# Last half of a fused attention and feed-forward kernel: the product with proj and the attention of the first half one slot sooner, each transpose directly behind its addition

## The chip, the core and the metric

The kernel runs on one core of a Trainium2 chip. The core has five engines with instruction streams of their own, which meet only through semaphores: PE (TensorE, matrix products into PSUM), DVE (VectorE), ACT (ScalarE), POOL (GpSimd) and SP (SyncE), which issues most of the DMAs. ACT issues four DMAs as well, at the very end. The metric is the device time of one execution in microseconds (us). Lower is better.

## The reference

```python
x = L0_attn_x                                   # (8, 1024, 256) float32
xn = _layernorm(x)                              # over the last axis, no weights
# attention, 16 heads of 16 channels, no softmax
qkv = xn @ qkv_w + qkv_b
q, k = l2norm(q), l2norm(k)                     # over the 16 channels of a head
kv  = einsum('bhnd,bhne->bhde', k, v)           # 16x16 for each head and batch
out = einsum('bhnd,bhde->bhne', q, kv)          # heads joined again: (8, 1024, 256)
attn = out @ proj_w + proj_b
# feed-forward, 256 -> 1024 -> 256
ffn = relu(xn @ W1 + b1) @ W2 + b2
return x + attn + ffn
```

## The kernel before

The 8 batches of 1024 tokens are worked through in 16 halves of 512 tokens; half `s` is the half `u = s % 2` of batch `b`. Every float32 factor is split into a high and a low part of type fp32r, and a product is three matmuls (`product`, L1006 to L1008): high by high, low by high, high by low. So most tiles come as a pair `_hi`, `_lo`: ACT makes the high part (L460, L523) and DVE subtracts it to get the low one (L677, L818).

The feed-forward part of a half runs over 8 chunks `j` of the 1024 inner channels. `ffn_up(j)` multiplies into `w_bank[j % 2]`; ACT takes the relu as `h_hi` (`h_high`), DVE the rest as `h_lo` (`h_low`); `ffn_down(j)` multiplies these by W2 into the output banks. PE's order is one list of slots written by hand: slot `j` holds `ffn_up(j + 2)`, then `ffn_down(j)`, then what else stands at that `j`. In the last half (`ahead` is false) `ffn_down` is `ffn_down_last`, 12 matmuls with 256 columns into `o_bank[0]`, `o_bank[1]` and `v_bank[0]`.

The attention has no softmax, so the tokens are summed first. `gather` (slot 2) accumulates xn^T k in `g_bank`, `key_value` multiplies it by the v weights into `kv_bank`, and DVE masks it to the blocks of the heads (`mask_kv`, L827 to L833 and L677). `project` multiplies that by proj into `g_bank`; `m_high` on ACT and `m_low` on DVE split the result into `m_hi` and `m_lo`. `attend(b, u, banks)` multiplies m by the transposed q of a half; one signal (`o_ready`) follows each of its two channel chunks.

In the last half `attend(b, 0, w_bank)` puts the attention of the batch's first half into the two `w_bank`s, which `ffn_up` no longer needs by then. It waits for `h_lo_done` of all 8 chunks, since `h_low` reads these banks, for `m_lo_done` and for `qT_lo_done`. After slot 7, `attend_last` adds the attention of the second half to the feed-forward sums in the output banks.

At the end DVE finishes both halves. For the first: `add_attention` (L845) adds the two `w_bank`s to what ACT had laid down of the feed-forward part, `spread_y` (L857) transposes 32x32 blocks into `y_rows`, `add_rows` (L863) adds them to x in `y_sb`. ACT then issues four stores (L668) of 128 KB each, one after the other; each covers 32 partitions in short pieces. For the second half: `add_last` (L871) adds the three output banks to `y_sb` as they come ready, and SP issues a store of 256 KB (L350) and two of 128 KB (L353). SP waits for all the stores before the kernel ends.

All five programs follow the same walk over the halves (`all_batches`). Six batches run in a loop on each engine; the first and the last are written out, so what is conditional on `ahead` or `last` touches only the last half.

Of the kernel before, what the change touches and what calls it, by code (L numbers as in the profile page):

```python
# [50 lines left out]
KC = C // P  # L51
# [11 lines left out]
def build(nc, x, qkv_w, qkv_b, proj_w, proj_b, w1, b1, w2, b2, out):  # L63
# [6 lines left out]
    with ctx:  # L70
# [140 lines left out]
        def is_first(s):  # L211
            return isinstance(s, int) and s == 0
# [245 lines left out]
        def _(act):  # L458
# [38 lines left out]
            def qk_out(s, u, t):  # L497

                wait(act, qk_ready, TILES * s + t + 1)
                wait(act, qk_ss_done, TILES * s + t - 1)  # L500
                nc.scalar.activation(qk_sq[:, t % 2, :], v_bank[t % 2][:], ACT.Square).then_inc(qk_sq_done, 1)  # L501
                if t == 0:
                    wait(act, q_transposed, s - 1)
                    wait(act, k_lo_done, s - 1)
                    if is_first(s):
                        act.wait_ge(wqk_ready, 1)
                    elif is_second(s):
                        act.wait_ge(w2_ready, PARTS)
                copy(qk[u][:, t, :], v_bank[t % 2][:]).then_inc(qk_copied, 1)
# [10 lines left out]
            def h_high(s, j):  # L520

                wait(act, h_ready, JC * s + j + 1)
                nc.scalar.activation(h_hi[:, j % RING, :], w_bank[j % 2][:], ACT.Relu).then_inc(h_done, 1)  # L523
# [92 lines left out]
            def half(b, s, u, last):  # L616
                ahead = not (last and u == 1)
                if not is_second(s):
                    h_high(s, 2)
                k_high(s, u)  # L620
                h_high(s, 3)
                if ahead:
                    qk_out(s + 1, 1 - u, 0)
                h_high(s, 4)
                if not last:
                    ln_sqrt(s + 2)
                    normalise(s + 2, u)
                if u == 1:
                    g_high(b)
                if not last:  # L630
                    xn_high(s + 2, u)
                h_high(s, 5)
                if ahead:
                    qk_out(s + 1, 1 - u, 1)
                h_high(s, 6)
                if is_second(s):
                    qT_high(0, 0)
                if ahead:
                    qT_high(s, u)
                    qk_out(s + 1, 1 - u, 2)  # L640
                h_high(s, 7)
                if ahead:
                    qk_out(s + 1, 1 - u, 3)
                    h_high(s + 1, 0)
                    qk_sqrt(s + 1)
                if u == 1:
                    m_high(b)
                if ahead:
                    h_high(s + 1, 1)
                    if u == 0:  # L650
                        yT_out(b, 0, 0)
                        yT_out(b, 0, 1)
                else:
                    qT_high(s, u)
                if not last:
                    xT_high(s + 2, u)
# [17 lines left out]
        def _(dve):  # L674
# [140 lines left out]
            def h_low(s, j):  # L815
                r = j % RING
                wait(dve, h_done, JC * s + j + 1)
                nc.vector.scalar_tensor_tensor(h_lo[:, r, :], w_bank[j % 2][:], 0.0, h_hi[:, r, :].bitcast(F32),  # L818
                                               ALU.max, ALU.subtract).then_inc(h_lo_done, 1)
# [5 lines left out]
            def mask_kv(b):  # L825
                wait(dve, kv_ready, b + 1)
                nc.vector.tensor_copy(kv[:], kv_raw[:, :, 0, :]).then_inc(kv_half_done, 1)  # L827
                wait(dve, kv_half_done, b + 1)
                nc.vector.tensor_tensor(kv[:], kv_raw[:, :, 1, :], kv[:], ALU.add).then_inc(kv_sum_done, 1)
                wait(dve, kv_sum_done, b + 1)  # L830
                nc.vector.tensor_tensor(kv[:], kv[:], head_mask[:], ALU.mult).then_inc(kv_masked, 1)
                wait(dve, kv_masked, b + 1)
                nc.vector.tensor_copy(kv_hi[:], kv[:]).then_inc(kv_hi_done, 1)  # L833
                wait(dve, kv_hi_done, b + 1)
                less(kv_lo[:], kv[:], kv_hi[:]).then_inc(kv_done, 1)
# [5 lines left out]
            def add_attention(b, k, last):  # L841

                wait(dve, o_ready, (2 * b * KC) + k + 1)
                wait(dve, yT_copied, KC * 2 * b + k + 1)
                nc.vector.tensor_tensor(yT[0][:, k, :], (w_bank if last else v_bank)[k][:], yT[0][:, k, :],  # L845
                                        ALU.add).then_inc(yT_added, 1)
# [87 lines left out]
            def half(b, s, u, last):  # L934
                ahead = not (last and u == 1)
                if not is_second(s):
                    if ahead:
                        xT_low(s + 1, 1 - u)
                    h_low(s, 2)
                divide(0, u, q_done)  # L940
                if is_second(s):
                    k_low(s, u)
                    h_low(s, 3)
                    transpose_q(s, u)
                else:
                    transpose_q(s, u)
                    h_low(s, 3)
                    k_low(s, u)
                if not last:
                    variance(s + 2, b + 1, u)  # L950
                h_low(s, 4)
                if ahead:
                    sum_squares(s + 1, 0)
                if not last:
                    spread(s + 2)
                if u == 1:
                    g_low(b)
                if not last:
                    transpose_x(s + 2)
                h_low(s, 5)  # L960
                if ahead:
                    sum_squares(s + 1, 1)
                else:
                    mask_kv(b)
                h_low(s, 6)
                if is_second(s):
                    qT_low(0, 0)
                if ahead:
                    qT_low(s, u)
                    sum_squares(s + 1, 2)  # L970
                    if u == 1:
                        mask_kv(b)
                h_low(s, 7)
                if ahead:
                    sum_squares(s + 1, 3)
                    bound(s + 1)
                    h_low(s + 1, 0)
                    norms(s + 1)
                if u == 1:
                    m_low(b)  # L980
                if ahead:
                    h_low(s + 1, 1)
                    divide(1, 1 - u, k_done)
                else:
                    qT_low(s, u)

            def end(b, last):
                for k in range(KC):
                    add_attention(b, k, last)
                for k in range(KC):  # L990
                    spread_y(b, 0, k)
                if last:
                    add_rows(b)
                    add_last(b)
                    return
                for k in range(KC):
                    spread_y(b, 1, k)
# [5 lines left out]
        def _(pe):  # L1003
# [199 lines left out]
            def half(b, s, u, last):  # L1203
                ahead = not (last and u == 1)
                for j in range(JC):
                    if j + AHEAD < JC:
                        ffn_up(s, u, j + AHEAD)
                    elif ahead:
                        ffn_up(s + 1, 1 - u, j + AHEAD - JC)
                    ffn_down(s, b, u, j, last)  # L1210
                    if j == 6 and not ahead:
                        pe.wait_ge(h_lo_done, JC * (s + 1))
                        attend(b, 0, w_bank)
                    if j == 1 and ahead:
                        query_key(s + 1, 1 - u, 0, b)
                    if j == 2:
                        gather(s, b, u)
                    if j == 3 and ahead:
                        query_key(s + 1, 1 - u, 1, b)
                    if j == 4 and ahead:  # L1220
                        query_key(s + 1, 1 - u, 2, b)
                    if j == 5 and ahead:
                        query_key(s + 1, 1 - u, 3, b)
                    if j == (4 if ahead else 3) and u == 1:
                        if isinstance(b, int) and b == 0:
                            pe.wait_ge(wvp_ready, 2)
                        key_value(b)
                    if j == (6 if ahead else 5) and u == 1:
                        project(b)

            def end(b, last):
# [27 lines left out]
```

## Time and profile before

| | us |
|---|---|
| median of 3 runs | 575.96 (575.56 to 576.06) |
| the profiled execution | 576.76 |
| its span, first to last instruction | 575.0 |
| PE busy | 560.1 (97%) |
| DVE busy | 416.6 (72%) |
| ACT busy | 282.6 (49%) |
| mean granted clock of PE | 0.997 of full speed |

A span is one execution as the hardware profiler saw it. A row of the timeline gives a start, a duration, the engine, the line and the operation. Matmuls are pipelined, so the start of one lies before the end of the one ahead of it: 0.39 us is the duration of a matmul of 512 columns, and one starts every 0.23 us. ACTq and SPq are the queues in which these engines issue DMAs; the duration of such a row is the issue and not the transfer. "To landing" counts from the start of the issue to the completion signal. Queue q10 is ACT's, q1 is SP's.

### The profile page before, as it was taken

To read this page: it belongs to the slowest core of one execution; us is meant where nothing else is said; L and a number is where in the kernel's file an instruction comes from. 1 tells how busy PE (TensorE), PEld (TensorE's weight loads), DVE (VectorE), ACT (ScalarE), POOL (GpSimd) and SP (SyncE) were. 2 spreads that over 40 slices of the span, in tenths; PEclk is the share of its full clock that TensorE was granted. 3 is DMA by queue.
4 is the path that set the end of the run, shared out by engine and by line. 5 is a ranking of instruction groups with operands and counts; after the bars stand their busy time and mean duration, and the time that the engine had idled before them with its cause. 6 is when DMAs were issued, how large, how long until landed. Compare 5 with 4: busy or idle time off the path is not lost.

```text
span 575.0 us, 8950 instructions
## 1 busy us (share of the span) xinstructions
PE 560.1 (97%) x2722; PEld 474.6 (83%) x2722; DVE 416.6 (72%) x807; ACT 282.6 (49%) x516; POOL 119.8 (21%) x147
## 2 busy tenths in 40 slices
PE   7999988999999999999999999999999999999995
PEld 6788767888888888888888888888888888888895
DVE  6888668767787677868678596776778767783744
ACT  3487273455535554355633645445554555533420
POOL 2338022310242010520205202132024301050100
PEclk9999999999999999999999999999999999999998
DMA  8303235144333536135451453514434252515323
GB/s 284 120 36 73 42 82 99 34 101 81 85 70 80 103 60 113 17 85 94 85 94 20 85 94 84 82 32 98 80 90 65 43 103 37 92 22 90 89 38 74
DMA packets 141398, 45.36 MB, mean 79 GB/s; under 512 B 133314, under 2 KB 136386, under 8 KB 141380
## 3 DMA queue, kind: packets, MB, share of 16 engines
q1 hardware_dynamic: 139264, 44.61, 38.4%
q10 hardware_dynamic: 2116, 0.53, 0.5%
q8 instruction: 9, 0.15, 0.1%
q14 instruction: 9, 0.07, 0.1%
HBM read 20.98 MB, written 8.39 MB: 51 GB/s over the span
## 4 chain that ended last, share of the span: by engine, by line
PE 84%; DVE 6%; SPq 5%; ACT 1%; DMA 1%; issue 1%; DVEq 0%; ACTq 0%
PE o_bank L1006 10%; PE o_bank L1007 10%; PE o_bank L1008 10%; PE w_bank L1008 9%; PE w_bank L1006 9%; PE w_bank L1007 9%; PE v_bank L1006 6%; PE v_bank L1007 6%; PE v_bank L1008 5%; SPq L305 5%; PE g_bank L1006 3%; PE g_bank L1008 3%; PE g_bank L1007 3%; DMA qT_lo<-blocks 1%; PE kv_bank L1127 1%
## 5 line engine op out<-in xcount | busy, mean ns | idle before, releaser
L818 DVE SCALAR_TENSOR_TENSOR h_lo<-w_bank,h_hi 128x512 fp32r<-128x512 f32 x128 | 87.4, 683 | 37.6 <-ACT h_hi L523 36.1
L523 ACT ACTIVATE h_hi<-w_bank 128x512 fp32r<-128x512 f32 x128 | 76.5, 597 | 72.4 <-PE w_bank L1008 70.4
L1006 PE MATMUL w_bank<-xT_hi,w_hi 128*128 128x512 f32 x254 | 99.9, 393 | 1.5 <-DVE h_lo L818 1.5
L1008 PE MATMUL w_bank<-xT_hi,w_lo 128*128 128x512 f32 x254 | 100.0, 394 | 0.0
L1007 PE MATMUL w_bank<-xT_lo,w_hi 128*128 128x512 f32 x254 | 99.7, 393 | 0.0
L368 POOL TENSOR_TENSOR xn_lo<-xn,xn_hi 128x256 fp32r<-128x256 f32 x60 | 44.6, 743 | 242.8 <-ACT xn_hi L460 239.3
L1006 PE MATMUL o_bank<-h_hi,w_hi 128*128 128x512 f32 x240 | 94.9, 395 | 0.0
L1007 PE MATMUL o_bank<-h_lo,w_hi 128*128 128x512 f32 x240 | 94.7, 395 | 0.0
L1008 PE MATMUL o_bank<-h_hi,w_lo 128*128 128x512 f32 x240 | 94.6, 394 | 0.0
L383 POOL TENSOR_TENSOR y_sb<-y_sb,y_rows 128x256 f32<-128x256 f32 x56 | 53.0, 951 | 127.6 <-DVE y_rows L857 108.1
L501 ACT ACTIVATE qk_sq<-v_bank 128x512 f32<-128x512 f32 x64 | 38.4, 599 | 77.9 <-PE v_bank L1008 76.8
L785 DVE TENSOR_REDUCE qk_v<-qk_sq 128x32 f32<-128x512 f32 x64 | 43.4, 681 | 33.5 <-ACT qk_sq L501 33.3
L1006 PEld LDWEIGHTS w_bank<-xT_hi,w_hi 128*128 128x128 f32 x254 | 47.7, 188 | 11.7 <-DVE h_lo L818 2.1
L1008 PEld LDWEIGHTS w_bank<-xT_hi,w_lo 128*128 128x128 f32 x254 | 47.7, 188 | 10.2
L1007 PEld LDWEIGHTS w_bank<-xT_lo,w_hi 128*128 128x128 f32 x254 | 47.7, 188 | 9.3
L1007 PEld LDWEIGHTS o_bank<-h_lo,w_hi 128*128 128x128 f32 x240 | 46.9, 195 | 9.4
L1006 PEld LDWEIGHTS o_bank<-h_hi,w_hi 128*128 128x128 f32 x240 | 46.5, 194 | 9.5
L1008 PEld LDWEIGHTS o_bank<-h_hi,w_lo 128*128 128x128 f32 x240 | 46.7, 195 | 9.2
L1006 PE MATMUL v_bank<-wqk_hi,xT_hi 128*128 128x512 f32 x128 | 50.6, 396 | 1.7 <-issue 1.5
L1007 PE MATMUL v_bank<-wqk_lo,xT_hi 128*128 128x512 f32 x128 | 50.3, 393 | 0.0
L1008 PE MATMUL v_bank<-wqk_hi,xT_lo 128*128 128x512 f32 x128 | 50.0, 391 | 0.0
L476 ACT ACTIVATE xn<-x_sb,ln_offset,ln_rstd 128x256 f32<-128x256 f32 x56 | 29.1, 590 | 27.9 <-DVE ln_offset L729 27.9
(183 smaller groups left out, 983.0 us busy)
## 6 DMA issues: line engine op xcount, KB each, us to landing
qT_lo<-blocks SPq DMA_DIRECT2D x256, 32.0 KB, 1.9
x_sb<-x SPq DMA_DIRECT2D x15, 512.0 KB, 3.8
y_sb<-x SPq DMA_DIRECT2D x60, 128.0 KB, 3.4
out<-y_sb SPq DMA_DIRECT2D x58, 128.0 KB, 2.7
xT_raw<-blocks SPq DMA_DIRECT2D x224, 32.0 KB, 1.9
y_sb<-w SPq DMA_DIRECT2D x4, 256.0 KB, 5.3
w_raw<-w SPq DMA_DIRECT2D x1, 768.0 KB, 9.5
x_sb<-x SPq DMA_DIRECT2D x2, 256.0 KB, 2.8
```

Source lines behind the costliest of these rows:

```text
L305: sp.dma_start(to_pairs[j * BLOCK:(j + 1) * BLOCK, :, g * run:(g + 1) * run], by_row[g * BLOCK:(g + 1) * BLOCK, j]).then_inc(moved, 16)
L368: nc.gpsimd.tensor_tensor(xn_lo[:, u, t, :], xn_of(s)[:, t, :], xn_hi[:, u, t, :].bitcast(F32), ALU.subtract).then_inc(xn_split_done, 1)
L383: nc.gpsimd.tensor_tensor(y_sb[:, u, t, :], y_sb[:, u, t, :], y_rows[:, u, t, :], ALU.add).then_inc(y_done, 1)
L476: done = nc.scalar.activation(to[:, t, :], x_sb[:, u, t, :], ACT.Identity, bias=ln_offset[:, t:t + 1], scale=ln_rstd[:, t:t + 1])
L501: nc.scalar.activation(qk_sq[:, t % 2, :], v_bank[t % 2][:], ACT.Square).then_inc(qk_sq_done, 1)
L523: nc.scalar.activation(h_hi[:, j % RING, :], w_bank[j % 2][:], ACT.Relu).then_inc(h_done, 1)
L785: nc.vector.tensor_reduce(qk_v[:, t, :], qk_sq[:, t % 2, :].rearrange("p (h d) -> p h d", d=D), AXIS.X, ALU.add).then_inc(qk_ss_done, 1)
L818: nc.vector.scalar_tensor_tensor(h_lo[:, r, :], w_bank[j % 2][:], 0.0, h_hi[:, r, :].bitcast(F32), ALU.max, ALU.subtract).then_inc(h_lo_do ...
L1006: nc.tensor.matmul(to, left[0], right[0], start=first, stop=False, skip_group_check=shared)
L1007: nc.tensor.matmul(to, left[0], right[1], start=False, stop=False, skip_group_check=shared)
L1008: return nc.tensor.matmul(to, left[1], right[0], start=False, stop=last, skip_group_check=shared)
L1127: nc.tensor.matmul(kv_raw[:, g, :, :], wv_hi[:, k, heads], g_parts[:, k, :, heads], start=g == 0 and k == 0, stop=False, skip_group_check= ...
```

## The change

In the last half alone, three programs are reordered.

```diff
@@ scalar: half
+                if not ahead:
+                    m_high(b)
                 h_high(s, 7)
...
-                if u == 1:
+                if u == 1 and ahead:
                     m_high(b)
@@ vector: half
+                if not ahead:
+                    m_low(b)
                 h_low(s, 7)
...
-                if u == 1:
+                if u == 1 and ahead:
                     m_low(b)
@@ vector: end
-                for k in range(KC):
-                    add_attention(b, k, last)
-                for k in range(KC):
-                    spread_y(b, 0, k)
+                if last:
+                    for k in range(KC):
+                        add_attention(b, k, last)
+                        spread_y(b, 0, k)
+                else:
+                    for k in range(KC):
+                        add_attention(b, k, last)
+                    for k in range(KC):
+                        spread_y(b, 0, k)
@@ tensor: half
-                    if j == 6 and not ahead:
+                    if j == 5 and not ahead:
                         pe.wait_ge(h_lo_done, JC * (s + 1))
                         attend(b, 0, w_bank)
...
-                    if j == (6 if ahead else 5) and u == 1:
+                    if j == (6 if ahead else 4) and u == 1:
                         project(b)
```

No instruction is added or taken away. On PE, this is the end of slot 4 of the last half and what follows it, before. The first row is the last matmul of `ffn_down(4)`, the next six are `ffn_up(7)`, and the last row begins `ffn_down(5)`.

```order
L1008 MATMUL v_bank0<-w2_hi,h_lo 128x256
L1006 MATMUL w_bank1<-xT_hi,w1_hi 128x512 [waits h_lo_done]
L1007 MATMUL w_bank1<-xT_lo,w1_hi 128x512
L1008 MATMUL w_bank1<-xT_hi,w1_lo 128x512
L1006 MATMUL w_bank1<-xT_hi,w1_hi 128x512
L1007 MATMUL w_bank1<-xT_lo,w1_hi 128x512
L1008 MATMUL w_bank1<-xT_hi,w1_lo 128x512
L1006 MATMUL o_bank0<-w2_hi,h_hi 128x256 [waits h_lo_done]
```

The same place on PE in the changed kernel:

```order
L1017 MATMUL v_bank0<-w2_hi,h_lo 128x256
L1015 MATMUL g_bank<-proj_hi,kv_hi 128x256 [waits kv_done]
L1016 MATMUL g_bank<-proj_lo,kv_hi 128x256
L1017 MATMUL g_bank<-proj_hi,kv_lo 128x256
L1015 MATMUL g_bank<-proj_hi,kv_hi 128x256
L1016 MATMUL g_bank<-proj_lo,kv_hi 128x256
L1017 MATMUL g_bank<-proj_hi,kv_lo 128x256
L1015 MATMUL w_bank1<-xT_hi,w1_hi 128x512 [waits h_lo_done]
```

The six matmuls of `project` now stand ahead of `ffn_up(7)` and `ffn_down(5)`. In the same way the 12 matmuls of `attend` have moved from behind `ffn_down(6)` to directly behind `ffn_down(5)`.

On ACT, the end of the program as a difference (`h_hi` rows are `h_high`, the row with `m_hi` is `m_high`):

```order
-L523 ACTIVATE h_hi<-w_bank 128x512 [waits h_ready] x3
+L523 ACTIVATE h_hi<-w_bank 128x512 [waits h_ready] x2
 L460 ACTIVATE m_hi<-g_bank 128x512 [waits m_ready]
-L460 ACTIVATE qT_hi<-qT_lo 128x512 [waits q_moved]
-L460 ACTIVATE qT_hi<-qT_lo 128x512
-L668 DMA out<-y_sb 32x16x64 [waits y_done]
-L668 DMA out<-y_sb 32x16x64 x3
+L523 ACTIVATE h_hi<-w_bank 128x512 [waits h_ready]
+L460 ACTIVATE qT_hi<-qT_lo 128x512 [waits q_moved]
```

One `h_high`, that of chunk 7, has gone behind `m_high`. The other rows only moved with it.

On DVE, the end of the program before, from `kv_lo` on; `h_lo` x2 are chunks 6 and 7:

```order
L677 TENSOR_TENSOR kv_lo<-kv,kv_hi 128x256 [waits kv_hi_done]
L818 SCALAR_TENSOR_TENSOR h_lo<-w_bank,h_hi 128x512 [waits h_done] x2
L677 TENSOR_TENSOR m_lo<-g_bank,m_hi 128x512 [waits m_hi_done]
L677 TENSOR_TENSOR qT_lo<-qT_lo,qT_hi 128x1024 [waits qT_hi_done]
L845 TENSOR_TENSOR xn_first<-w_bank,xn_first 128x512 [waits yT_copied,o_ready] x2
L857 STREAM_TRANSPOSE y_rows<-xn_first 128x512 [waits y_done,yT_added]
L857 STREAM_TRANSPOSE y_rows<-xn_first 128x512 [waits yT_added]
L863 TENSOR_TENSOR y_sb<-y_sb,y_rows 128x1024 [waits yT_spread,y_loaded0]
```

And in the changed kernel:

```order
L679 TENSOR_TENSOR kv_lo<-kv,kv_hi 128x256 [waits kv_hi_done]
L820 SCALAR_TENSOR_TENSOR h_lo<-w_bank,h_hi 128x512 [waits h_done]
L679 TENSOR_TENSOR m_lo<-g_bank,m_hi 128x512 [waits m_hi_done]
L820 SCALAR_TENSOR_TENSOR h_lo<-w_bank,h_hi 128x512 [waits h_done]
L679 TENSOR_TENSOR qT_lo<-qT_lo,qT_hi 128x1024 [waits qT_hi_done]
L847 TENSOR_TENSOR xn_first<-w_bank,xn_first 128x512 [waits yT_copied,o_ready]
L859 STREAM_TRANSPOSE y_rows<-xn_first 128x512 [waits y_done,yT_added]
L847 TENSOR_TENSOR xn_first<-w_bank,xn_first 128x512 [waits yT_copied,o_ready]
L859 STREAM_TRANSPOSE y_rows<-xn_first 128x512 [waits yT_added]
L865 TENSOR_TENSOR y_sb<-y_sb,y_rows 128x1024 [waits yT_spread,y_loaded0]
```

`m_low` now stands between the two `h_low`, and the first transpose between the two additions.

## Rows read from the trace of the kernel before

**Rows 1.** The page's chain of work that ended last, by engine.

```profile
PE 84%; DVE 6%; SPq 5%; ACT 1%; DMA 1%; issue 1%; DVEq 0%; ACTq 0%
```

**Rows 2.** Timeline of the queues: start, duration of the issue, queue, line.

```profile
545.31 10.87 SPq L305 DMA_DIRECT2D qT_lo<-blocks  x16
...
568.15 0.38 ACTq L668 DMA_DIRECT2D out<-y_sb  x1
...
568.75 0.38 SPq L350 DMA_DIRECT2D out<-y_sb  x1
...
569.65 1.36 ACTq L668 DMA_DIRECT2D out<-y_sb  x1
...
569.70 1.34 SPq L353 DMA_DIRECT2D out<-y_sb  x1
```

**Rows 3.** Stores: queue, count, KB each, median us to landing; last row: those of 569.65 and 569.70.

```profile
out<-y_sb SPq DMA_DIRECT2D x58, 128.0 KB, 2.7
...
out<-y_sb ACTq DMA_DIRECT2D x1, 128.0 KB, 2.2
...
out<-y_sb SPq DMA_DIRECT2D x1, 256.0 KB, 3.3
...
DMA to landing us min/median/max: 4.7/4.9/5.0
```

**Rows 4.** DMA queues, 569 to 575: packets, MB, share of 16 engines' time.

```profile
q10 hardware_dynamic: 2112, 0.52, 50.4%
q1 hardware_dynamic: 432, 0.52, 25.4%
```

**Rows 5.** Busy time of each engine by stretch, granted clock, DMA share, GB/s.

```profile
569.00:569.50 0.50, 0.16 (x2) 0.00 (x0) 0.35 (x2) 0.00 (x0) 0.00 (x0) 1.00 0.78 130
...
569.50:573.50 4.00, 0.00 (x0) 0.00 (x0) 0.12 (x1) 0.00 (x0) 0.00 (x0) 0.69 0.99 234
```

**Rows 6.** Timeline of PE: start, duration, line, operation.

```profile
556.68 0.39 PE L1006 MATMUL w_bank<-xT_hi,w_hi 128*128 128x512 f32 x1
...
559.50 0.28 PE L1006 MATMUL g_bank<-proj_hi,kv_hi 128*128 128x256 f32 x1
...
561.51 0.28 PE L1008 MATMUL v_bank<-w_hi,h_lo 128*128 128x256 f32 x1
561.81 0.47 PE L1006 MATMUL w_bank<-qT_hi,m_hi 128*128 128x512 f32 x1
...
568.88 0.28 PE L1008 MATMUL v_bank<-m_hi,qT_lo 128*128 128x256 f32 x1
```

**Rows 7.** Timeline of DVE; in brackets idle time before and its releaser.

```profile
555.71 0.42 DVE L677 TENSOR_TENSOR kv_lo<-kv,kv_hi 128x256 fp32r<-128x256 f32 x1
...
558.89 0.69 DVE L818 SCALAR_TENSOR_TENSOR h_lo<-w_bank,h_hi 128x512 fp32r<-128x512 f32 x1 [2.12 <-ACT h_hi L523]
561.02 0.69 DVE L677 TENSOR_TENSOR m_lo<-g_bank,m_hi 128x512 fp32r<-128x512 f32 x1 [1.44 <-ACT m_hi L460]
...
563.48 0.69 DVE L845 TENSOR_TENSOR xn_first<-w_bank,xn_first 128x512 f32<-128x512 f32 x1 [0.20 <-PE w_bank L1008]
564.88 0.69 DVE L845 TENSOR_TENSOR xn_first<-w_bank,xn_first 128x512 f32<-128x512 f32 x1 [0.71 <-PE w_bank L1008]
565.49 1.30 DVE L857 STREAM_TRANSPOSE y_rows<-xn_first 128x512 f32<-128x512 f32 x2
566.89 1.23 DVE L863 TENSOR_TENSOR y_sb<-y_sb,y_rows 128x1024 f32<-128x1024 f32 x1
...
569.20 0.42 DVE L871 TENSOR_TENSOR y_sb<-v_bank,y_sb 128x256 f32<-128x256 f32 x1
```

**Rows 8.** Timeline of ACT, its last rows that are no DMA.

```profile
558.25 0.60 ACT L523 ACTIVATE h_hi<-w_bank 128x512 fp32r<-128x512 f32 x1 [2.21 <-PE w_bank L1008]
560.39 0.60 ACT L460 ACTIVATE m_hi<-g_bank 128x512 fp32r<-128x512 f32 x1 [1.53 <-PE g_bank L1008]
560.88 1.14 ACT L460 ACTIVATE qT_hi<-qT_lo 128x512 fp32r<-128x512 f32 x2
```

## The prediction

> **What bounds the kernel now.** I read the chain of waits first. It is 84% PE [rows 1], and PE is busy 97% of the span (the table above), so as long as matmuls are left, every other engine is cover. The change adds and removes no matmul. So the question is whether it shortens a wait of PE, or the stretch behind the last matmul, in which PE is no longer the bound.
>
> Then the timeline of PE at the end. Between the last matmul of `ffn_down(6)` at 561.51 and the first of `attend` at 561.81 lie 0.30 us, where such matmuls otherwise start 0.12 apart: (561.51 - 559.50) / 17 = 0.118 for the 18 from `project` on. PE waits 0.18 us there. DVE shows for what: `m_lo` runs from 561.02 to 561.71, and `attend` starts 0.10 later [rows 6, 7]. PE's last matmul starts at 568.88 and DVE's last addition at 569.20; it ends at 569.62 [rows 6, 7].
>
> Behind that there is only DMA. SP issues its last store at 569.70, ACT its last one at 569.65 [rows 2]; they take 4.7 and 5.0 us to landing [rows 3], so they land at 574.40 and 574.65. The span ends at 575.0, 0.4 behind the later one. 5.4 of the 575 us are thus a tail without a matmul. Is that the price of one store? No: a store of SP takes 2.7 us as the median of 58, and ACT's first one, with nothing before it, took 2.2 [rows 3]. From 569.5 to 573.5 the 16 DMA engines are 0.99 busy [rows 5]. All the seven last stores stand in line there: the four of ACT, issued from 568.15 on [rows 2], with 2112 small packets and 50.4% of six us, and the three of SP with 432 packets and 25.4% [rows 4]. That is 3.02 + 1.52 = 4.55 us of work for all the engines together. It starts at about 569.1 (0.78 of 569.0 to 569.5 is busy [rows 5]), 0.95 us after ACT's first issue, and so is worked off at 573.65 at the earliest. The tail is bound by the amount that is left to store when PE ends, and two thirds of it belong to the first half, whose result is complete long before.
>
> **The change, part by part.**
>
> 1. `project` goes from behind `ffn_down(5)` to before `ffn_up(7)`. It takes the place at 556.68 instead of 559.50 [rows 6], 2.82 sooner. It needs `kv_lo`, which ends at 555.71 + 0.42 = 556.13 [rows 7]; 0.55 us are to spare. Cost 0, and a stall of PE for whatever `kv_lo` is later than that.
>
> 2. `ffn_up(7)` and `ffn_down(5)` slide back by the six matmuls of `project`, 6 x 0.118 = 0.7 us. `m_hi` on ACT moves with `project`: 560.39 - 2.82 = 557.57, and ends at 558.17. `h_hi` of chunk 7 moves from 558.25 to 558.95 [rows 8], so it doesn't wait for `m_hi` though it now stands behind it. On DVE `m_lo` runs from 558.20 to 558.89, `h_lo` of chunk 7 from 558.89 + 0.7 = 559.59 to 560.28 [rows 7]. No wait here either.
>
> 3. `attend` goes from behind `ffn_down(6)` to behind `ffn_down(5)`. Before, `ffn_down(5)` ended where `project` began, at 559.50; now it ends at 560.20. `attend` waits for three things. `m_lo` is there at 558.89, 1.3 us early: the old wait is gone. What is late next is `h_lo` of chunk 7, at 560.28. With the 0.10 us that the signal took before, `attend` starts at 560.38, and PE waits 0.18 us again, as much as before. The price of this wait lies between 0 (the signal is as fast as PE's own queue) and 0.5 (if ACT and DVE take 0.3 longer for that chunk, which is about half an operation of 0.60). I take 0.18, so the balance of PE is 0 and its last matmul still starts at 568.88. Behind `attend` stand the 24 matmuls of slots 6 and 7 and `attend_last`. The latter needs `qT_lo` of the second half: `qT_hi` follows `h_hi` at 559.55 (its moves were issued by 545.31 + 10.87 = 556.18 [rows 2]) and ends at 560.69, `qT_lo` takes 1.23 and is done at about 561.96, 4 us before it is needed.
>
> 4. `attend` is 561.81 - 560.38 = 1.43 us sooner, and so are both `o_ready`. The first addition moves from 563.48 to 562.05, just behind `qT_lo`. The second would start at 564.88 - 1.43 = 563.45 [rows 7].
>
> 5. The first transpose goes between them. Two transposes take 1.30 together [rows 7], so one 0.65 to 0.69. The first addition ends at 562.74, the transpose runs until 563.45 at the latest: it fits into the 0.71 us in which DVE waited for PE before the second addition [rows 7]. The second addition ends at 564.14, its transpose at about 564.85. `add_rows` started 0.10 behind the transposes (566.79 and 566.89 [rows 7]), so now at 564.95, and ends at 566.18 instead of 568.12: 1.94 us sooner, 1.43 from `attend` and 0.5 from the hidden transpose. The page "VectorE: DVE Perf Modes" of the Trainium skill, section "The DRAIN you can't avoid", speaks against this order: a DVE instruction doesn't start until the pipeline behind the one before is empty. Here the second addition and the transposes that didn't depend on it stand 565.49 - 564.88 = 0.61 apart with 0.69 of busy time each, so the trace shows some overlap where nothing is waited for. By the rule nothing is lost in the new order; by the rows up to 0.1 for each dependent pair, and that is in the times above.
>
> 6. ACT's four stores are issued from 566.2 on instead of 568.15. No other edit touches the tail. SP's first store comes 0.3 us sooner too, since `add_last` no longer stands behind `add_rows` when its first bank is ready; its last one stays at 569.70, bound by PE.
>
> **What the tail becomes.** The packets start 0.95 behind the first issue, now at 567.1. The 4.55 us of work would be done at 571.7 if nothing ran dry. SP's last store can't begin to move before about 569.70 + 0.95 = 570.65; by then ACT's 3.0 us of work, begun at 567.1, is nearly all out. So the end is that of a nearly undisturbed store of 128 KB: 2.2 us to landing at the least, 2.7 at the median, 3.3 as SP's 256 KB store took in the middle of the jam [rows 3]. That gives a landing at 571.9, 572.4 or 573.0, and with the 0.4 behind it a span of 572.3, 572.8 or 573.4. The gains are 2.7, 2.2 and 1.6 us. I take the median store's, 2.2: it is the row for the same queue and size, and it agrees with the work's end at 571.7 plus the 0.6 to 1.0 that landing took behind 573.65 before.
>
> The page "DMA: Bandwidth & Descriptors", section "Issuing engines are not separate DMA queues", says that DMAs from any engine run on the same 16 engines and interleave. The trace agrees: both queues' packets share the stretch in which the DMA share is 0.99 [rows 5]. Were the rings separate, ACT's load would not have slowed SP's last store, and the gain would be that of the second rival. The same page, section "Latency and other measured facts", adds that the completion of a write is shorter when HBM is lightly loaded; no row here separates that part.
>
> Sum: 576.76 of the profiled execution - 2.2 = 574.5. It lay 0.8 above the median of the runs, 575.96. From the median I get 573.7.
>
> **Rivals.**
>
> *The jam dissolves only in part.* ACT's last issue took 1.36 us against 0.38 for the first [rows 2]; if the four issues are slow by themselves, the last packets of the first half meet SP's last store. Then that one lands after the mean of 3.3 and 4.7, 4.0 us: 573.7, span 574.1, gain 0.9, time 575.0. Against it: SP's issues were as slow at the same moment (1.34), so the delay is shared and comes from the jam.
>
> *The last store's 4.7 us are its own.* Then only ACT's later landing falls away: the end goes from 574.65 to 574.40, gain 0.25, time 575.7. For it speaks that the clock of the tail is set by a row that does not move (569.70). Against it are 2.2 and 2.7 for stores of the same size.
>
> *PE stalls more: slower.* `attend` now comes one slot behind `ffn_up(7)` where it came two behind, and the way over ACT and DVE has no slack left. The place is the `h_lo` wait; every us there moves PE's last matmul and SP's last store with it. With the gain of the tail at 2.2, it decides from 2.2 us on; to be 1.2 slower in the end it would need 3.4. The nearest rows make 0.5 of it at most. Only if the tail gave nothing, and `kv_lo` and `h_lo` both came an operation late (0.42 + 0.69 us over their slack), would the time be 576.8.
>
> *It doesn't do what it says.* If `y_done` came less than 1 us sooner (an addition that waits for `qT_lo`, with 0.09 us to spare in step 4), the tail would still shrink by nearly as much. This is within the first rival.
>
> **Chances.** The measurement of this kernel can tell about 0.2%, 1.15 us, from no change. The forecast, a gain of 1.6 to 2.7, has 0.74. The first rival, 0.6 to 1.6, has 0.15, of which I count 0.1 as faster. The second has 0.08. The slower case has 0.03. That makes 0.85 faster (with what lies above 2.7), 0.12 within 0.2% and 0.03 slower. The range goes from 2.7, the bound, with 0.35 us for the scatter of the runs (half of what lies between 575.56 and 576.06, and a little more), 572.9, to the first rival's 575.0.
>
> **What would show it.** PE: `project` starting near 556.7 without a gap, `attend` near 560.4 behind a gap of about 0.2, `attend_last` ending where it did, at 569.2. DVE: the first transpose between the additions, `add_rows` ending near 566.2. ACTq: the first store near 566.2 and the last by 568.5. DMA: the engines busy from 567.1 on, well below 0.9 after 571, and SP's last store 2.2 to 3.3 us to landing. The forecast is wrong if that one still takes over 4 us, if the last landing is not SP's, or if PE's end has moved by more than 0.3.

## The result and the profile after

| | before | after |
|---|---|---|
| median of 11 runs, us | 576.38 (575.56 to 577.11) | 574.49 (573.93 to 575.21) |
| the profiled execution | 576.76 | 573.93 |
| its span | 575.0 | 572.2 |

The ratio is 0.9968, with an interval from 0.9960 to 0.9976. The changed kernel is faster by 1.84 us, with 1.4 to 2.3 in the interval; the forecast was 2.2. The time of 574.49 lies 0.8 above the forecast 573.7: half of that is the smaller gain, and the other half is that the kernel before itself came out at 576.38 here and not at the 575.96 that the forecast started from. The two spans are 2.8 us apart, which is more than the change made. About 1.05 of that was there long before the last half: the first sums of squares of q and k on DVE start at 34.12 in one trace and at 32.98 in the other, the first matmul of the third half's `gather` at 107.34 and 106.30, and at the end of slot 4 of the last half the two traces are still 1.05 apart. So times of the two traces are compared from a common place: the end of `ffn_down(4)`, 556.68 before [rows 6] and 555.63 after.

The timeline of PE after: start, duration, line, operation.

```profile
555.63 0.28 PE L1015 MATMUL g_bank<-proj_hi,kv_hi 128*128 128x256 f32 x1
...
556.32 0.39 PE L1015 MATMUL w_bank<-xT_hi,w_hi 128*128 128x512 f32 x1
...
559.02 0.28 PE L1017 MATMUL v_bank<-w_hi,h_lo 128*128 128x256 f32 x1
559.27 0.51 PE L1015 MATMUL w_bank<-qT_hi,m_hi 128*128 128x512 f32 x1
559.62 0.39 PE L1016 MATMUL w_bank<-qT_lo,m_hi 128*128 128x512 f32 x1
...
567.81 0.28 PE L1017 MATMUL v_bank<-m_hi,qT_lo 128*128 128x256 f32 x1
```

`project` starts without a gap. `attend` starts 3.64 us behind the common place; before it was 561.81 - 556.68 = 5.13 [rows 6], so it is 1.49 sooner. In front of it there is again a gap, 0.25 from start to start where 0.12 is usual, and its first matmul holds the next back by 0.35 instead of 0.23. The last matmul lies 12.18 us behind the common place, and 12.20 before: PE has gained nothing.

The same stretch on DVE:

```profile
557.15 0.69 DVE L679 TENSOR_TENSOR m_lo<-g_bank,m_hi 128x512 fp32r<-128x512 f32 x1 [1.42 <-ACT m_hi L460]
558.52 0.69 DVE L820 SCALAR_TENSOR_TENSOR h_lo<-w_bank,h_hi 128x512 fp32r<-128x512 f32 x1 [0.68 <-ACT h_hi L523]
559.56 1.23 DVE L679 TENSOR_TENSOR qT_lo<-qT_lo,qT_hi 128x1024 fp32r<-128x1024 f32 x1 [0.35 <-ACT qT_hi L460]
560.98 0.69 DVE L847 TENSOR_TENSOR xn_first<-w_bank,xn_first 128x512 f32<-128x512 f32 x1 [0.19 <-PE w_bank L1017]
561.70 0.71 DVE L859 STREAM_TRANSPOSE y_rows<-xn_first 128x512 f32<-128x512 f32 x1
562.38 0.69 DVE L847 TENSOR_TENSOR xn_first<-w_bank,xn_first 128x512 f32<-128x512 f32 x1
563.11 0.72 DVE L859 STREAM_TRANSPOSE y_rows<-xn_first 128x512 f32<-128x512 f32 x1
563.93 1.23 DVE L865 TENSOR_TENSOR y_sb<-y_sb,y_rows 128x1024 f32<-128x1024 f32 x1
...
568.13 0.42 DVE L873 TENSOR_TENSOR y_sb<-v_bank,y_sb 128x256 f32<-128x256 f32 x1 [0.29 <-PE v_bank L1017]
```

The first addition and the first transpose fill the 1.40 us between the starts of the two additions; before, 0.71 of them were idle [rows 7]. `add_rows` ends at 565.16, 9.53 behind the common place instead of 11.44: 1.91 sooner.

The issues of the stores, ACT's four together and the last of SP:

```profile
565.18 2.24 ACTq L670 DMA_DIRECT2D out<-y_sb  x4
...
567.48 0.38 SPq L350 DMA_DIRECT2D out<-y_sb  x1
567.91 1.48 SPq L353 DMA_DIRECT2D out<-y_sb  x2
```

And how SP's two stores of 128 KB (line 353) fared, from the view of that line:

```profile
DMA to landing us min/median/max: 3.0/3.1/3.2
```

The last of the two, issued at 568.69, is the one with 3.0 us to landing, against 4.7 [rows 3]. I call the time from the end of DVE's last addition to the end of the span the **tail**, and the time from the end of `add_rows` to the end of DVE's last addition the **lead** that the first half's stores have. Before, the lead was 1.50 us and the tail 5.41 (with the span of 575.03, which is 575.0 when rounded); now they are 3.39 and 3.65. The tail is 1.76 us shorter, and that is the whole gain. The other tails below are taken from spans rounded to 0.1 us, so each is good to 0.05.

### The profile page after: what moved, and what is told of

It is laid out like the page before. It is cut to its first block, busy times and chain, and to the rows that moved or that the text cites. A ratio compares the mean times of both kernels' runs of the same rounds, so it can differ in the third digit from the quotient of the medians.

```text
span 572.2 us, 8950 instructions
## 1 busy us (share of the span) xinstructions
PE 560.6 (98%) x2722; PEld 475.7 (83%) x2722; DVE 415.2 (73%) x807; ACT 282.7 (49%) x516; POOL 119.4 (21%) x147
## 4 chain that ended last, share of the span: by engine, by line
PE 84%; DVE 6%; SPq 5%; ACT 2%; issue 1%; DMA 1%; DVEq 0%; ACTq 0%
PE o_bank L1015 10%; PE o_bank L1016 10%; PE o_bank L1017 10%; PE w_bank L1017 9%; PE w_bank L1015 9%; PE w_bank L1016 9%; PE v_bank L1015 6%; PE v_bank L1016 6%; PE v_bank L1017 6%; SPq L305 5%; PE g_bank L1015 3%; PE g_bank L1017 3%; PE g_bank L1016 3%; PE kv_bank L1136 1%; DVE ln_parts L707 1%
```

## The experiments

All ratios are to the kernel before, run beside it on the same chip. The diffs are against the changed kernel, and the minus lines are its lines, if nothing else is said.

**e1: the slots alone.**

```diff
-                if last:
-                    for k in range(KC):
-                        add_attention(b, k, last)
-                        spread_y(b, 0, k)
-                else:
-                    for k in range(KC):
-                        add_attention(b, k, last)
-                    for k in range(KC):
-                        spread_y(b, 0, k)
+                for k in range(KC):
+                    add_attention(b, k, last)
+                for k in range(KC):
+                    spread_y(b, 0, k)
```

> The changed kernel with the two additions and then the two transposes on DVE, as before; project and attend stay one slot sooner. Jam theory (the tail is as long as the stores of both halves take to drain, so it shrinks by 0.9 us for each us that the first half's result comes sooner, 1.76 / 1.94 in the profiles of the two kernels): the addition of x and y_rows ends 1.4 us sooner instead of 1.94, the gain over the kernel before is 1.3 us, ratio 0.9977. Floor theory (with the first half out of the way SP's last store is the end by itself, and 1.4 us are already enough): the gain is the whole 1.8 us of the changed kernel, ratio 0.9968, and SP's last store lands 3.2 us after its issue.

Ratio 0.9971 (0.9961 to 0.9982). The interval holds the values of both theories, but the profile tells them apart. These rows are `add_rows` and DVE's last addition; the span is 573.8:

```profile
565.72 1.23 DVE L865 TENSOR_TENSOR y_sb<-y_sb,y_rows 128x1024 f32<-128x1024 f32 x1
...
569.46 0.42 DVE L873 TENSOR_TENSOR y_sb<-v_bank,y_sb 128x256 f32<-128x256 f32 x1 [0.29 <-PE v_bank L1012]
```

The lead is 2.93, the tail 3.92. It has not reached the 3.65 of the changed kernel, and SP's two stores of 128 KB took 3.4 and 3.6 us to landing instead of 3.2 at most, so there was no floor yet. For 1.43 us more lead than before the tail gave 1.49.

**e2: the transposes alone** (the kernel before with the `if last` branch that e1 takes out).

> The kernel before with the first transpose between the two additions; project and attend stay where they were. Jam theory: the first transpose fits into the 0.71 us in which DVE waited for PE, the addition of x and y_rows ends 0.5 us sooner, the gain is 0.45 us, ratio 0.9992, and e1 and e2 add up to the changed kernel. Floor theory: 0.5 us here as well, but e1 and e2 together give more than the changed kernel. If the transposes cost more behind their additions than they hide: no gain.

Ratio 0.9998 (0.9990 to 1.0007): the expected 0.9992 is inside, no change as well; the runs can't tell. In the profile DVE places the transpose between the additions as in the changed kernel (additions at 562.70 and 564.10, transpose at 563.43), the lead grows to 1.96, and the tail is 4.96: 0.45 less, the expected amount. That is a single profile, and the runs neither confirm nor refute it.

**e3: `m_high` and `m_low` behind chunk 7 again**, with PE's order as changed.

```diff
-                if not ahead:
-                    m_high(b)
                 h_high(s, 7)
...
-                if u == 1 and ahead:
+                if u == 1:
                     m_high(b)
```

and the same for `m_low`.

> The changed kernel with m_high and m_low behind h_high and h_low of chunk 7 again on ACT and DVE; PE's order stays changed. If this order matters as the row arithmetic has it: m_lo ends 0.65 us later than attend now starts, PE waits 0.8 us instead of 0.13, its last matmul and SP's last store are 0.65 later and so is the first half's result; the gain over the kernel before falls from 1.8 to 1.1 us, ratio 0.998. If ACT and DVE have cover there: no difference from the changed kernel, ratio 0.9968.

Ratio 0.9986 (0.9977 to 0.9994). PE's last matmul of `ffn_down(5)` and the first of `attend`:

```profile
559.28 0.28 PE L1013 MATMUL v_bank<-w_hi,h_lo 128*128 128x256 f32 x1
560.18 0.48 PE L1011 MATMUL w_bank<-qT_hi,m_hi 128*128 128x512 f32 x1 [0.62 <-issue]
```

The gap is 0.90 instead of 0.25. From `h_lo` of chunk 6 to the last matmul it takes 13.40 us, against 12.78 in the changed kernel (555.03 to 567.81). So PE lost 0.62. The gain fell from 1.8 to 0.8 us, with 0.3 to 1.3 in its interval; the expected 1.1 is inside, and so is what the profile gives, 1.0 (a tail of 573.2 - 569.43 = 3.77, and PE 0.62 later). So the new order on ACT and DVE is what keeps the slot move free for PE.

**e4: banks that are free.** `v_bank[1]` was last read for q and k of the half and `kv_bank` by `mask_kv`, so `attend` need not wait for chunk 7.

```diff
-                        pe.wait_ge(h_lo_done, JC * (s + 1))
-                        attend(b, 0, w_bank)
+                        attend(b, 0, [v_bank[1], kv_bank])
...
-                nc.vector.tensor_tensor(yT[0][:, k, :], (w_bank if last else v_bank)[k][:], yT[0][:, k, :],
+                nc.vector.tensor_tensor(yT[0][:, k, :], ([v_bank[1], kv_bank] if last else v_bank)[k][:], yT[0][:, k, :],
```

> The changed kernel with the attention of the first half put into v_bank[1] and kv_bank, which nothing reads any more, so that attend doesn't wait for h_low of chunk 7. If that wait is all that holds PE: attend starts 0.12 behind the last matmul of ffn_down(5) instead of 0.25, and its first matmul takes 0.23 instead of 0.35, so PE ends 0.25 us sooner, the first half's result 0.2 sooner, and the time is 0.25 us less than the changed kernel's: gain over before 2.1, ratio 0.9964. Rival: the first matmul with new operands is slow by itself and the gap stays; same as the changed kernel.

```profile
559.79 0.28 PE L1017 MATMUL v_bank<-w_hi,h_lo 128*128 128x256 f32 x1
559.91 0.39 PE L1015 MATMUL v_bank<-qT_hi,m_hi 128*128 128x512 f32 x1
560.14 0.39 PE L1016 MATMUL v_bank<-qT_lo,m_hi 128*128 128x512 f32 x1
```

Gap and slow first matmul are both gone, so both belonged to the wait, and from `h_lo` of chunk 6 to the last matmul it takes 12.53, 0.25 less. The tail is 3.62. The ratio, 0.9971 (0.9960 to 0.9982), is too coarse to show 0.25 us.

**e5 and e6: no stores by ACT**, in the changed kernel and in the kernel before. The last batch's first half is computed and not written.

```diff
-                for q in range(GROUPS):
-                    rows = slice(q * BLOCK, (q + 1) * BLOCK)
-                    act.dma_start(out_blocked[2 * b][q], by_block(y_sb[rows, 0])).then_inc(stored[0], 16)
```

SP waits for four stores fewer at the end.

> The changed kernel without ACT's four stores: the last batch's first half is computed but not written, so this is the floor of the tail. From DVE's last addition to the end of the span it is 3.65 us in the changed kernel and 5.41 in the kernel before. Jam theory with something left of the jam: SP's last store lands after 2.2 to 2.7 us instead of 3.0, the tail is 3.0 to 3.3, the gain over the kernel before 2.1 to 2.4, ratio 0.996. If the 3.0 us are the store's own: the tail stays at 3.6, ratio 0.9968 as for the changed kernel.

> The kernel before without ACT's four stores (the last batch's first half isn't written). If they are all that made its tail longer, its tail equals that of the changed kernel without them, 3.0 to 3.3 us against 5.41 with them, ratio 0.996, and PE ends at the same place in both. If the second half's stores have a price of their own in the old order (add_last behind add_rows): the tail stays above that of e5 by 0.3.

Ratios 0.9937 (0.9917 to 0.9956) and 0.9945 (0.9928 to 0.9963). DVE's last addition ends at 569.15 and 569.25 and the spans are 571.4 and 571.7, so the tails are 2.25 and 2.45. Without ACT's stores, SP's two of 128 KB land like this in e5:

```profile
DMA to landing us min/median/max: 1.7/1.9/2.0
```

Both tails are shorter than I had expected (3.0 to 3.3), so the floor is far lower than I had put it. Of the 5.41 us of the tail before, 3.0 came from the other half's stores, and in the changed kernel 1.4 us of that are still left. The two tails also differ by 0.20, near the 0.3 of the second theory, with no store of the first half in either. In e6 `add_last` stands behind `add_rows`, and SP's first store is issued at 568.38, 0.87 ahead of the end of DVE's last addition; in e5 it is issued at 568.08, 1.07 ahead of it. So about 0.2 of the 1.76 that the tail lost by the change may come from this earlier start of SP's own stores, and not from the first half's.

**e7: two queues.** Two of the four stores of the first half go out by SP. The lines ahead of the gap are ACT's, and those behind it stand at the head of SP's part of `end`.

```diff
-                for q in range(GROUPS):
+                for q in range(GROUPS // 2):
                     rows = slice(q * BLOCK, (q + 1) * BLOCK)
                     act.dma_start(out_blocked[2 * b][q], by_block(y_sb[rows, 0])).then_inc(stored[0], 16)
...
+                sp.wait_ge(y_done, TILES * 2 * b + 1)
+                for q in range(GROUPS // 2, GROUPS):
+                    of = slice(q * BLOCK, (q + 1) * BLOCK)
+                    sp.dma_start(out_blocked[2 * b][q], by_block(y_sb[of, 0])).then_inc(stored[0], 16)
```

> The changed kernel with two of the four stores of the first half issued by SP instead of ACT, so that the four issues take half as long (2.24 us on one queue). If the DMA engines' time for the many small packets is the limit: share of the engines 0.97 to 0.99 either way, last landing and time as in the changed kernel within 0.1 us, ratio 0.9968. If the pace of the issues is: the packets are done up to 1 us sooner and the tail falls to 3.3 us, ratio 0.996.

Ratio 0.9954 (0.9939 to 0.9970). DVE's last addition ends at 568.76, the span at 571.4: a tail of 2.64, 1.0 shorter than the changed kernel's with the same lead. The theory that the engines' time is the limit falls: it had the tail unchanged within 0.1. The theory of the issues' pace had the right sign, but it expected a tail of 3.3. The ratio alone does not set e7 apart from the changed kernel, whose interval overlaps; the tail does, and e9 repeats it below. One microsecond among the small packets (PE, PEld, DVE, ACT, POOL, granted clock, DMA share, GB/s), in the changed kernel:

```profile
566.50:567.50 1.00, 1.00 (x11) 1.00 (x10) 0.73 (x2) 0.00 (x0) 0.00 (x0) 1.00 0.98 156
```

and in e7:

```profile
567.00:568.00 1.00, 1.00 (x10) 1.00 (x10) 1.00 (x2) 0.00 (x0) 0.00 (x0) 1.00 1.13 223
```

The engines were as good as full in the first, and still moved 43% more in the second. So a busy share, which even goes above 1 here, is the time that packets were under way and not an amount of work. The queue lines of 564.5 to 575 show it too. ACT's queue in the changed kernel, and then in e7:

```profile
q10 hardware_dynamic: 2112, 0.52, 30.4%
```

```profile
q10 hardware_dynamic: 1056, 0.26, 11.2%
```

That is 10.5 x 16 x 30.4% / 2112 = 24 ns for one small packet when they all go through ACT's queue, and 18 ns for ACT's half of them in e7. SP's queue had 29.0% there, 3.05 us, of which I put 1.49 down to its own three stores (their 15.7% of 9.5 us in e5); that leaves 24 ns for its half of the small ones. The sum of both queues is 4.2 us of engine time instead of 4.7. The packets begin at 566.1 in the changed kernel and at 566.25 in e7. From 567.0 to 567.5 e7 moves 230 GB/s and in the half microsecond after that 215, while the changed kernel stays at 150 to 156 until 567.5, drops to 129 after that, has 255 from 568.0 to 568.5, and 152 in the half microsecond behind it. How much of the 1.0 us is the smaller sum and how much the earlier fast pace, these numbers don't say.

Nor does e7 tell two queues from earlier issues, for it changed both. Its four issues end at 566.35:

```profile
565.39 0.96 ACTq L674 DMA_DIRECT2D out<-y_sb  x2
```

```profile
565.38 0.87 SPq L351 DMA_DIRECT2D out<-y_sb  x2
```

In the changed kernel they end at 567.42. The pace jumps there half a microsecond behind that end, when the packets of the fourth store are due; the first packets, too, came 0.52 behind the end of the first issue (565.56 and 566.08):

```profile
567.70:567.90 0.20, 0.20 (x4) 0.19 (x2) 0.14 (x1) 0.00 (x0) 0.00 (x0) 1.00 0.75 106
567.90:568.10 0.20, 0.19 (x2) 0.00 (x0) 0.00 (x0) 0.00 (x0) 0.00 (x0) 1.00 1.18 247
```

In e7 the fast pace is there from 567.0 on, 0.65 behind the end of its last issue. I come back to this behind e11.

**e8: `add_rows` and the stores in two pieces**, on top of e4.

```diff
-                nc.vector.tensor_tensor(y_sb[:, 0], y_sb[:, 0], y_rows[:, 0], ALU.add).then_inc(y_done, 1)
+                for n in range(PAIRS):
+                    tiles = slice(n * PAIR, (n + 1) * PAIR)
+                    nc.vector.tensor_tensor(y_sb[:, 0, tiles], y_sb[:, 0, tiles], y_rows[:, 0, tiles],
+                                            ALU.add).then_inc(y_done, 1)
```

ACT issues four stores of 64 KB behind each piece.

> The kernel of e4 (free banks, no wait for h_low of chunk 7) with add_rows in two pieces of two tiles each and eight stores of 64 KB instead of four of 128 KB, so that the first ones are issued 0.6 us sooner. Jam theory with the slope seen so far beyond a lead of 2.9 us (0.27 us of tail for 0.46 us of lead): the tail falls by 0.2 to 0.3 from 3.65, and with the 0.25 us of PE from e4 the gain over the kernel before is 2.3 us, ratio 0.996. If eight issues cost what they bring (they take 3.2 us in all on one queue), the tail is 3.65 as in e4, ratio 0.9964; if they make it longer, over 0.997.

Ratio 0.9974 (0.9960 to 0.9987), and a tail of 573.2 - 569.64 = 3.56 beside 3.62 in e4. The expected 0.2 to 0.3 less did not come.

```profile
565.74 4.39 ACTq L673 DMA_DIRECT2D out<-y_sb  x8
```

Eight issues took 4.39 us instead of the 3.2 I had counted on, and the DMA engines ran partly dry between them (share 0.50 from 567 to 568, against 0.98 above). With half the size the issues set the pace there.

**e9: e4 and e7 together, e10: the kernel before with e7's sharing, e11: the changed kernel with all four stores by SP, e12: the changed kernel again.**

> e4 and e7 together: no wait of attend for h_low of chunk 7, and the first half's four stores issued two by ACT and two by SP. If the two are independent: PE ends 0.25 us sooner as in e4, and the tail from DVE's last addition to the end is 2.6 us as in e7; gain over the kernel before 2.8 + 0.25 = 3.0 us, ratio 0.9948. If e7's tail came from the place of its stores in that run alone, the tail is back at 3.6 and the ratio at 0.9964.

> The kernel before with only the issue of the first half's four stores shared between ACT and SP. Queue theory (one queue moves these small packets at 155 GB/s with the engines at 0.99, two queues faster): the jam is shorter even in the old order, tail 3.9 us instead of 5.41, gain 1.5 us, ratio 0.9974, though SP's own three stores now stand behind two issues of 0.4 us. If sharing helps only where SP's own stores don't come in between: no gain, or 0.4 us slower, ratio 1.0 to 1.0007.

> The changed kernel with all four stores of the first half issued by SP, ACT issues none. If the pace is that of one queue, whichever it is: the first half's packets move at 155 GB/s again and are done by about 3.4 us after they begin, and since SP's own stores stand behind them in the same queue instead of sharing the engines with them, the tail is 3.0 us. If it is ACT's queue that is slow: SP moves them at the pace of e7, the tail is 2.6 us or less. If what counts is only the sum of all packets: 3.65 us as in the changed kernel.

> The changed kernel itself, unchanged, on the same chip as e9 to e11, so that they can be set against it: ratio 0.9968, tail 3.65 us by all theories. A tail that differs by more than 0.3 us would say how far one profiled execution can be trusted.

| | ratio (interval) | lead | tail |
|---|---|---|---|
| e9 | 0.9947 (0.9934 to 0.9961) | 3.40 | 2.65 |
| e10 | 0.9992 (0.9983 to 1.0001) | 1.49 | 4.83 |
| e11 | 0.9959 (0.9946 to 0.9973) | 3.40 | 3.62 |
| e12 | 0.9961 (0.9947 to 0.9974) | 3.40 | 3.59 |

e9 does what its parts do: 12.54 us from `h_lo` of chunk 6 to the last matmul, tail 2.65. Its median of 573.12 is the lowest of the kernels that write all of the output; that of e12, run beside it, is 574.12. The intervals overlap a little, and the profiles say 0.25 + 0.94 = 1.2 us. e12's tail is 0.06 from that of the changed kernel's first profile, and e9's 0.01 from e7's. So a difference of 1.0 between two tails is far outside what these profiles scatter; one of 0.1 is not.

e10 shows where sharing helps little. The tail fell by 0.6, not by 1.5. SP's own stores stood behind two issues, and issuing them took longer:

```profile
567.72 0.80 SPq L354 DMA_DIRECT2D out<-y_sb  x1
568.56 1.87 SPq L357 DMA_DIRECT2D out<-y_sb  x2
```

The last of them was issued at 569.70, 1.43 behind the end of DVE's last addition; in the kernel before it was 0.08 behind it.

e11 answers whether ACT's queue is the slow one: SP's is just as slow when it has all four stores. It begins with the small packets as ACT's did, with 0.98 of the engines at 153 GB/s, and reaches 240 GB/s only from 568.5 on, 1.7 us behind its first packets.

```profile
567.00:568.00 1.00, 1.00 (x11) 1.00 (x10) 0.51 (x1) 0.00 (x0) 0.00 (x0) 1.00 0.98 153
```

The 3.0 us that I had drawn from the theory of one queue's pace didn't come: the tail is 3.62, the value expected if only the sum of all packets counts, which e7 contradicts. What agrees with all of these runs is the end of the fourth issue.

```profile
565.90 2.21 SPq L351 DMA_DIRECT2D out<-y_sb  x4
```

It ends at 568.11, and the jump from 118 to 256 GB/s comes at 568.6, again half a microsecond later. The same holds in e1, e3, e4 and e12: in the 0.2 us ahead of a point 0.5 behind the end of the fourth issue the pace is 106 to 128 GB/s in all six profiles, and in the 0.2 us after it 247 to 259. And the tails sort by it. In the changed kernel, e3, e4, e11 and e12 the fourth issue ends 1.12 to 1.17 ahead of the end of DVE's last addition, and the tails are 3.59 to 3.77; in e7 and e9 it ends 2.4 ahead, and they are 2.64 and 2.65. But in these runs the two queues and the early issues always go together. No run issues four stores as early from one queue, so whether the second queue does anything beyond ending the issues sooner stays open, and so does why the first three stores alone move at only 155 GB/s with the engines at 0.98.

## Why the prediction was right, and which term was off

**The wait of PE.** By step 3 it should stay 0.18 us; the rows say 0.13 of gap and 0.12 in the first matmul, 0.25 together, as before (0.18, and 0.08 as the next matmul started at 562.12). The balance of 0 was right, to 0.02 us. e3 confirms that the order on ACT and DVE was needed for it, and e4 that the wait was for `h_lo` of chunk 7.

**`attend`, the transposes, `add_rows`.** Steps 2 to 5 put `attend` 1.43 sooner and the end of `add_rows` 1.94 sooner. The trace has 1.49 and 1.91. e1 and e2 split the tail's gain: the slots alone brought 1.49, the transposes alone 0.45. Together they are 1.94, and the change had 1.76. It looks as if the tail gave less for more lead: 1.04 us per us from a lead of 1.50 to 2.93, and 0.6 from there to 3.39. But the 0.27 us behind the second figure are a difference of two single profiles, and with 0.1 us of doubt in it this flattening is likely rather than shown.

**The tail: this term was mis-sized.** I took the median store's 2.7 us to landing for the last one, and a gain of 2.2. It took 3.0, the tail lost 1.76, and the runs say 1.84. That the forecast came as near was in part luck: two things in that step were wrong, and they partly cancelled. The floor was too high: a store of that size lands in 1.7 to 2.0 us when only SP's three are under way (e5), not in 2.2 to 2.7. And "the end is that of a nearly undisturbed store" did not hold. ACT's packets were indeed nearly all out at the moment at which the forecast let SP's last store begin to move, 569.70 + 0.95 = 570.65 or 569.6 in the trace after: 59 of 2112 were left. But SP's own were not: 390 of its 432 packets and 0.44 of its 0.52 MB still stood there (queue lines of 569.60 to 571.5). SP issued its first store at 567.48, and its first packet came at 569.03, 1.55 later, while ACT's packets filled the engines (share 0.94 from 568.5 to 569.03); without them it was 0.87 later (e5, 568.08 and 568.95). From there SP's packets took 2.3 us to be written instead of 1.6 (to 571.37, and to 570.54 in e5). The two delays, 0.7 and 0.7, are the 1.4 us of jam that are left in the tail. So the last store had to share with SP's own first two, which the first half's had held back, and my account had no term for that. The sign I had set for it failed too: the engines' share was to be well below 0.9 after 571, which is 569.95 here, and it was 1.04 from 570.0 to 570.5. Behind this stands the sum of 4.55 us of engine time, which I took for an amount of work that is done without a pause. ACT's packets took 4.4 us from the first to the last (566.1 to 570.5), with a share of 0.82 from 567.5 to 568.0, and e7 moved the same packets with 0.5 us less of engine time.

**Smaller slips.** Step 6 had SP's first store 0.3 sooner; from the common place it was 0.2. "The 0.6 to 1.0 that landing took behind 573.65" is 0.75 to 1.0 by the rows. 576.76 - 2.2 is 574.56 and 575.96 - 2.2 is 573.76, each put down 0.06 too low. In the rival of the PE stall the case in which the tail gives nothing adds up to 575.96 + 0.42 + 0.69 = 577.1 and not to 576.8. None of them moves the range.

**The rivals.** "The jam dissolves only in part" was the nearer one for the mechanism, though not for its size: the gain was above its 1.6. "The last store's 4.7 us are its own" falls with e5 and e6, in which it took 1.7 and 1.9. "PE stalls more" came true only in e3, where it was built in: 0.62 us of stall, and a gain that shrank from 1.8 to 0.8. The rule of the Trainium skill on the DRAIN (page "VectorE: DVE Perf Modes", section "The DRAIN you can't avoid") spoke against the new order of the transposes. It cost almost nothing: each starts 0.03 to 0.04 us after its addition ends.

## What to carry to other kernels

Look at what is left to store when the compute engine ends, and move the parts that are complete earlier out of the way before anything else; here 1.9 us of lead were worth 1.8 us of time without a single matmul saved. If many small packets go out at the end, look at when the last of their issues ends, and share the issues between the two issuing engines, as long as neither of them has its own last stores due in between: here that took 1.0 us off the tail in e7, and only 0.6 in e10, where SP's own stores stood behind them. And don't add up the DMA engines' busy shares as if they were work: take the time of a store that is alone from a run that leaves the others out.

## What the runs showed of the hardware

- Four stores of 256-byte pieces, issued one after the other by ACT or by SP, moved at 151 to 160 GB/s for more than a microsecond with the engines at 0.97 to 0.99 busy. They reached 227 to 255 GB/s only 1.6 to 1.9 us after the first packet, 0.5 us behind the end of the fourth issue. With two issued by each engine, 216 to 230 GB/s were there within a microsecond (e7, e9). SP's stores of 1 and 2 KB pieces moved at 362 GB/s when nothing else was under way (e5, 569 to 570, share 1.01).
- SP's first packet came 0.87 us behind its issue with nothing else under way (e5), and 1.55 us behind it when ACT's packets filled the engines (the changed kernel).
- An SP store of 128 KB landed 1.7 to 2.0 us after its issue when only SP's own stores were under way (e5, e6), and 4.3 to 4.7 us in the jam of the kernel before.
- Issuing a store of 128 KB took 0.33 to 0.51 us with nothing but SP's own stores or no store under way (e5, and ACT's first two in the changed kernel), and up to 1.36 us in the jam [rows 2]. An engine that issues stores can be held up by the stores of the other: SP's last two issues took 0.43 and 0.33 us in e5, and 0.74 and 0.70 in the changed kernel, which differs only in ACT's four stores.
- The first matmul behind a semaphore wait held the next back by 0.35 us instead of 0.23, and that went away with the wait (e4).
